# First attention of a four-part layer stack: the turned results, the state's chain and the turned states take other places in the step

## The reference

```
x: 16 batches of 256 tokens, 128 wide; 16 heads of 8
x = layernorm(x) * ln_w + ln_b
q, k, v = x @ Wq + bq, x @ Wk + bk, x @ Wv + bv      # per head
q, k = q / |q|, k / |k|
state = q
for _ in range(2):
    sim = einsum('bqhd,bkhd->bqhk', state, k)
    att = softmax(sim)
    state = einsum('bqhk,bkhd->bqhd', att, v)
return residual + state @ Wo + bo
```

## Time and profile before

| | |
|---|---|
| median of 3 runs | 1747.52 us (1744.76 to 1750.48) |
| profiled execution | 1759.47 us, span 1757.7 us |
| PE busy | 1489.7 us, 85% of the span |
| DVE busy | 1189.0 us, 68% |
| ACT busy | 1000.8 us, 57% |
| POOL busy | 785.2 us, 45% |
| first attention: first and last s0 or s1 | 59.2 to 559.7 us of the span |

### The profile page before, as it was taken

How to read it: one execution, slowest core, us unless ns; L and a number is a source line. 1 busy time by engine, 2 the same in 40 slices (tenths; PEclk the granted TensorE clock), 3 DMA queues, 4 the chain that set the end, 5 groups by cost and what they waited for, 6 DMA issues and landing times. The chain is left out here.

```text
span 1757.7 us, 37146 instructions
## 1 busy us (share of the span) xinstructions
PE 1489.7 (85%) x12057; PEld 1147.2 (65%) x12057; DVE 1189.0 (68%) x3253; ACT 1000.8 (57%) x1682; POOL 785.2 (45%) x1008
## 2 busy tenths in 40 slices
PE   2599999999999587999169998999899999689997
PEld 1467767767766466899046666666666666478886
DVE  2367777767766555999556777777777766556676
ACT  1377777777776254777126565665656666333332
POOL 8765464685662343998562334343333220100111
PEclk9899999999999788999569999999999999789999
DMA  5000000010010110222211111111111111000000
GB/s 192 21 20 19 16 19 17 25 32 19 25 35 19 33 58 12 73 68 64 77 42 35 35 35 40 31 35 33 33 33 33 31 30 30 1 1 7 12 12 18
DMA packets 75074, 60.29 MB, mean 34 GB/s; under 512 B 17088, under 2 KB 71104, under 8 KB 74560
## 3 DMA queue, kind: packets, MB, share of 16 engines
q1 hardware_dynamic: 70848, 50.21, 10.0%
q0 software_dynamic: 4096, 8.40, 1.7%
HBM read 20.01 MB, written 13.37 MB: 19 GB/s over the span
## 5 line engine op out<-in xcount | busy, mean ns | idle before, releaser
L1274 DVE TENSOR_REDUCE a_qt<-a_ps_d 128x2 fp32r<-128x512 f32 (+1 forms) x384 | 263.6, 689 | 140.8 <-PE a_ps_d L1059 96.3
L537 ACT ACTIVATE a_p<-a_ps_s 128x1024 f32<-128x1024 f32 x256 | 263.1, 1029 | 63.8 <-PE a_ps_s L395 59.4
L638 DVE TENSOR_REDUCE a_qt<-a_ps_d 128x2 fp32r<-128x512 f32 x256 | 171.6, 685 | 105.8 <-PE a_ps_d L406 105.5
L799 POOL TENSOR_TENSOR a_rn<-a_ss,a_half 128x16 f32<-128x16 f32 x64 | 185.9, 2913 | 1.4
L1186 ACT ACTIVATE a_pg<-a_ps_s 128x1024 f32<-128x1024 f32 x128 | 131.8, 1031 | 12.5 <-PE a_ps_s L1033 7.4
L1059 PE MATMUL a_ps_d<-a_kpad,a_qs 128*128 128x512 f32 x256 | 126.2, 493 | 13.6 <-DVE a_qt L1274 12.5
L406 PE MATMUL a_ps_d<-a_kpad,a_qs 128*128 128x512 f32 x256 | 119.7, 471 | 15.5 <-DVE a_qt L638 13.9
L413 PE MATMUL a_ps_o<-a_p,a_v 128*32 128x256 f32 x2048 | 125.3, 384 | 1.0 <-ACT a_p L537 1.0
L1024 PE MATMUL a_ps_a<-ident,a_qt 128*128 128x128 f32 x512 | 107.1, 291 | 10.8 <-ACT a_qsm L1180 8.0
L1505 POOL COPY a_v<-a_vt 128x64 f32<-128x64 f32 x64 | 15.4, 240 | 212.8 <-PE a_ps_o L1136 212.8
L1180 ACT CAST a_ks<-a_ps_a 128x256 fp32r<-128x256 f32 x128 | 47.6, 372 | 110.0 <-PE a_ps_a L1024 101.7
(11 more groups left out here) (359 smaller groups left out, 4280.1 us busy)
## 6 DMA issues: line engine op xcount, KB each, us to landing
a_kpad<-a_ks SPq DMA_DIRECT2D x512, 32.0 KB, 1.8
a_kpad<-a_kq SPq DMA_DIRECT2D x256, 32.0 KB, 1.9
f_xin<-xs SPq DMA_DIRECT2D x39, 128.0 KB, 2.1
ys<-f_yout SPq DMA_DIRECT2D x39, 128.0 KB, 2.1
w<-in_w SPq DMA_DIRECT2D x2, 2304.0 KB, 11.3
out_x<-X SPq DMA_DIRECT2D x8, 256.0 KB, 2.3
xs<-f_zero SPq DMA_DIRECT2D x15, 128.0 KB
wgu<-in_wgu SPq DMA_DIRECT2D x1, 1152.0 KB
```

The source lines that it names most:

```text
L537: nc.scalar.activation(probs[:, u % 2, 2 * c:2 * c + 2, :, :].rearrange("p a b c -> p (a b c)"), ps_s[:, n % 2, :], ACT.Exp).then_inc(exp_ ...
L638: nc.vector.tensor_reduce(qt2[:, k % 2, 2 * part:2 * part + 2, SHIFT], bank(k, f"m{part}")[:, :].rearrange("p (a b) -> p a b", b=S), AX.X, ...
L799: nc.gpsimd.tensor_tensor(rn[:, part * c:(part + 1) * c], ss[:, part * c:(part + 1) * c], half[:, 0:c], ALU.pow).then_inc(rn_ready, 1)
L1274: nc.vector.tensor_reduce(dst, src, AX.X, ALU.max, negate=True).then_inc(d_done, 1)
```

## The change

Three pieces of step k move; no instruction is added or removed.

- On TensorE T goes ahead of s1 (still behind s0 and qp).
- On TensorE O goes from behind m3 to behind KQ, ahead of vp and m2.
- On VectorE the chain of O goes from behind m3 to behind m1, ahead of vp, the two moments, m2 and m3. `D_ORDER` follows: O now takes its bank between m1 and vp (or m2).

```
--- before.py
+++ after.py
@@ -199,7 +199,7 @@
     FIRST, LAST = -3 * NG, UNITS + 3 * NG - 1
 
     A_ORDER = ("T", "KQ", "xT", "yT", "zT")
-    D_ORDER = ("qp", "m0", "lg", "place", "kp", "m1", "vp", "m2", "m3", "O", "op")
+    D_ORDER = ("qp", "m0", "lg", "place", "kp", "m1", "O", "vp", "m2", "m3", "op")
     KQ_RING = NG + 1
 
     def steps(eng):
@@ -444,8 +444,6 @@
                 if projects:
                     pe.wait_ge(a_done, a_count(k - 1, "xT"))
                     project(st, 0, "qp")
-                if unit(k):
-                    score_chunk(st, 1, kq[:, k % KQ_RING, 1, :])
                 if a_live(k, "T"):
                     pe.wait_ge(d_done, d_count(k - 1, "m3"))
                     wait_a(st, "T")
@@ -455,6 +453,8 @@
                     if unit(k - 3):
                         last = stack(lambda t: qt2[:, (k - 3) % 2, t * G:(t + 1) * G, :], 1)
                     last.then_inc(a_full, 1)
+                if unit(k):
+                    score_chunk(st, 1, kq[:, k % KQ_RING, 1, :])
                 if unit(k - 1) or unit(k - 4):
                     wait(pe, o_copied, attends(k - 1))
                     if unit(k - 4):
@@ -492,12 +492,6 @@
                     wait_a(st, "KQ")
                     stack(lambda t: kt[:, nb % 2, t * H + g * G:t * H + (g + 1) * G, :], 0)
                     stack(lambda t: qt[:, nb % 2, t * H + g * G:t * H + (g + 1) * G, :], 1).then_inc(a_full, 1)
-                if projects:
-                    project(st, 2, "vp")
-                maxima(st, 2)
-                if unit(k - 3):
-                    score_chunk(st, 3, qs2[:, S:2 * S])
-                maxima(st, 3)
                 if d_live(k, "O"):
                     wait_d(st, "O")
                     pe.wait_ge(o_copied, attends(k))
@@ -505,6 +499,12 @@
                     for n in range(live.start, live.stop, P):
                         last = nc.tensor.transpose(bank(k, "O")[:, n:n + P], ot[:, n:n + P], ident[:, :])
                     last.then_inc(d_full, 1)
+                if projects:
+                    project(st, 2, "vp")
+                maxima(st, 2)
+                if unit(k - 3):
+                    score_chunk(st, 3, qs2[:, S:2 * S])
+                maxima(st, 3)
                 if r == 2 and batch(b + 3):
                     pe.wait_ge(z1_ready, b + 4)
                     wait_a(st, "xT")
@@ -718,16 +718,6 @@
                     if not batch(b - 3):
                         last.then_inc(stats_b, 1)
                 maxima(1)
-                if r == 3 and batch(b + 3):
-
-                    wait(dve, v_ready, st.at(lambda k: NG * (k // NG + 2)))
-                    projected(st, 2, "vp", vt[:, (b + 3) % 2, :, :])
-                if r == 1 and batch(b - 3):
-                    moments(st, "new", 0, mv_b).then_inc(stats_b, 1)
-                if r == 0 and batch(b + 3):
-                    moments(st, "x", TPB, mv_a).then_inc(stats_a, 1)
-                maxima(2)
-                maxima(3)
                 if d_live(k, "O"):
 
                     dve.wait_ge(d_full, d_count(k, "O"))
@@ -758,6 +748,16 @@
                         dve.wait_ge(d_done, d_count(k, "O"))
                         nc.vector.tensor_tensor(new[:, :, 2 * HD:3 * HD], state[:, :, :],
                                                 new[:, :, 0:HD].bitcast(F32), ALU.subtract).then_inc(qt2_ready, 1)
+                if r == 3 and batch(b + 3):
+
+                    wait(dve, v_ready, st.at(lambda k: NG * (k // NG + 2)))
+                    projected(st, 2, "vp", vt[:, (b + 3) % 2, :, :])
+                if r == 1 and batch(b - 3):
+                    moments(st, "new", 0, mv_b).then_inc(stats_b, 1)
+                if r == 0 and batch(b + 3):
+                    moments(st, "x", TPB, mv_a).then_inc(stats_a, 1)
+                maxima(2)
+                maxima(3)
                 if r == 2 and batch(b - 2):
 
                     dve.wait_ge(d_full, d_count(k, "op"))
```

More of the change, by code:

```diff
@@ L494, in _ @@
                     stack(lambda t: qt[:, nb % 2, t * H + g * G:t * H + (g + 1) * G, :], 1).then_inc(a_full, 1)
[L495 to L500, removed]
                 if d_live(k, "O"):
@@ L720, in _ @@
                 maxima(1)
[L721 to L730, removed]
                 if d_live(k, "O"):
```

## The result

Before 1748.62 us (median of 4 runs, 1744.76 to 1750.48), after 1772.16 us (4 runs, 1771.08 to 1775.52): ratio 1.0141, 95% interval 1.0118 to 1.0164. The change makes the kernel 23.5 us slower; the prediction was 1769.0, 21.5 us slower, with a range of 1756 to 1781.

The account below looks back on a forecast made before the run. The prediction saw a loop of waits, with VectorE holding three T in four. 1.96 - 0.63 + 0.10 = 1.43 us per batch, times 15 batches, gave 21.5 us on a 1747.5 median: 1769.0 us, range 1756 to 1781.

Parts of the forecast that it names:

- s1 goes onto the loop: Between T and attend on TensorE: s1's four loads, hidden before, now cost 0.49 us per step, 1.96 per batch.
- m0 to T: Time from m0's start to T's in each step: 21.43 us per batch predicted, before 22.06.
- End 5.40, T 5.52: At r = 3: VectorE's reductions end 5.40 us after m0 and T starts at 5.52; before 5.79.
- T's copy comes no later with respect to T: ScalarE behind T: s1's chunk comes later, but T's copy was not to be delayed relative to T; no size given.
- the 0.63 us of gain: Between m0 and T: 0.63 us gained per batch from gaps in which VectorE waited.
- The moments on GpSimd: Moments behind O's chain reach GpSimd later; the scaling then delays r = 2's first reduction by 0.1 us per batch.
- few tenths: Three batches where scatters fill GpSimd: the later `stats_a` may add a few tenths of a us to each.
- The sum: Steps 4 to 63: 1.43 us more per batch, counted alike for 15 batches, 21.5 us.
- Faster: Rival: TensorE holds T in most steps, so T comes 0.49 us earlier per step; 1732 us, chance 0.07.
- Same: Rival: m0 to T shrinks by the price of s1, leaving time within 0.3%; 1750 us, chance 0.09.
- Much slower through GpSimd: Rival: late moments make the scaling delay r = 2's first reduction by 1 us or more; 1783 us, chance 0.08.
- a fall of the clock: Rival: longer TensorE idle time drops the clock to 1.2 GHz over the stage; about 1910 us, chance 0.01.

Follow-up runs that it names:

- e1: T alone moved ahead of s1 in the kernel before, O, its chain and `D_ORDER` unmoved: 1764.18 us, ratio 1.0098.
- e5: The changed kernel with the transposes zT right behind m0 and their copy ahead of the third exponential: 1770.49 us, ratio 1.0131.
- e6: The changed kernel with s3 ahead of m2: 1764.92 us, ratio 1.0101.
- e3: The changed kernel with VectorE's two moments ahead of O's chain again: 1767.03 us, ratio 1.0114.
- e4: The changed kernel with s1 ahead of T again and the moments ahead of O's chain: 1757.24 us, ratio 1.0057.
- e2: The changed kernel with s1 ahead of T again, so only O and its chain move: 1765.92 us, ratio 1.0108.
- e8: The kernel before with T cut in two, unit k-3's two transposes ahead of s1, the others behind: 1742.61 us, ratio 0.9972.
- e7: The changed kernel with moments ahead of O's chain, s3 ahead of m2, T cut in two around s1: 1747.37 us, ratio 0.9993.

## Why the prediction was right, point by point

*s1 goes onto the loop, 0.49 per step.* Right, and shown by e1: T to m0 grew from 2.45 to 2.92, at r = 3 to 0 from 2.50 to 2.98; 11.76 - 9.85 = 1.91 per batch for 1.96 predicted.

*m0 to T.* At r = 0 and 1 the walk along VectorE held: 5.26 and 5.29 predicted, 5.19 and 5.16 measured; T follows a reduction by 0.06 and not by 0.12, the lower of my two bounds. At r = 2 and 3 it failed: 5.36 and 5.52 predicted, 5.68 and 5.98 measured. The step of the prediction that failed at r = 3 is "End 5.40, T 5.52": I followed VectorE only and left out the other things for which T waits, the bank `ps_a`, and with it ScalarE's queue. "T's copy comes no later with respect to T" was beside the point; what stood ahead of T on ScalarE mattered (e5, e6). At r = 2 "op" was followed rightly: in the changed kernel it starts 453.75 - 449.43 = 4.32 after m0 instead of 4.00, 0.25 of it from the late first reduction. So the 0.63 us of gain came out as 0.05.

*The moments on GpSimd.* The mechanism was right, the size in ordinary batches 0.25 instead of 0.10. GpSimd itself kept to the forecast: `stats_b` comes 445.35 - 441.35 = 4.00 after its m0 and the scaling 4.26 behind it. What was off is the loop that hides it: r = 0 and r = 1 together took 16.20 us and not 16.43, so m0 of r = 2 was there sooner. The "few tenths" for the batches with scatters were 0.66 in steps 38 and 42 (first reduction 2.65 and 2.66 after m0, before 1.99 and 2.00), while in step 54 the wait shrank from 2.26 to 1.07. By e3 the moments' place is worth 4.7 us of the 23.5, with overlapping intervals, and by e4 against e2 8.7 where s1 doesn't lengthen the loop.

*The sum.* An ordinary batch costs 1.86 us more, not 1.43. That the total of 21.5 still came near 25.4 for the stage and 23.5 in the median is in part luck, two errors against each other: the first two batches cost 1.23 and 1.58, the last two 1.29 and 0.55, steps 52 to 55 nothing (-0.08), and I had counted all 15 alike; the two batches of steps 36 to 43 cost 2.29 and 3.61, the second with 1.3 of half clock.

*Rivals.* "Faster" needed m0 to T to shrink by 0.49 per step; it shrank by 0.01. "Same" falls with it. "Much slower through GpSimd" has the right mechanism at a quarter of its price. What I had not foreseen as a rival is that O's place costs in itself, 9.6 us in e4: 0.33 per batch at r = 2 through "op", which the prediction had seen but set against the 0.49 of s1, and 0.43 at r = 3 through m2's wait, s3 and the exponential, which it had not. The two halves don't add: 16.5 and 18.2 alone, 23.5 together. Per ordinary batch it is 1.40, 1.18 and 1.86. About a quarter of a microsecond of the difference lies at r = 2, where the scaling is less late in the longer loop (first reduction at 0.79 instead of 1.05); about 0.2 each lie at r = 1 and r = 3 and were not followed.

## What to carry to other kernels

A block that an engine does while it waits for another is free only in that place: before moving it behind the wait, ask whether the wait itself gets shorter by the block's length. When a step of a hand-ordered pipeline is moved, follow every semaphore of its new neighbours, also those of banks (m2 behind O's bank held s3, an exponential and a copy back), and the small signals that stand behind it for a third engine. Of a block that waits for two things, cut off the part that waits for the earlier one and do that first (e8), after a look at whose copy still holds its bank.

## What the runs showed of the hardware that was not expected

In the profiled execution of the changed kernel the clock fell once between step 4 and step 64. In step 42 (r = 2, with scatters) the weight loads stood still for 1.99 us ahead of O, and soon after TensorE was granted 1.2 GHz for a little over 3 us:

```profile
415.88 0.42 PEld L500 LDWEIGHTS a_ps_d<-ident,a_ot 128*128 128x128 f32 x4 [1.99 <-DVE a_qt L638]
```

```profile
378.00:382.00 4.00, 1.80 (x13) 1.28 (x12) 3.06 (x10) 1.36 (x2) 3.52 (x4) 1.00 0.18 44
414.00:418.00 4.00, 1.79 (x12) 1.39 (x11) 3.39 (x12) 0.99 (x3) 3.24 (x4) 1.00 0.16 41
418.20:421.40 3.20, 3.20 (x16) 2.83 (x15) 1.37 (x3) 2.92 (x5) 0.81 (x2) 0.50 0.06 17
```

The first row is step 38, which has the same wait of 1.99 us, the second is step 42. In both the matmul rows cover 1.8 of 4.00 us at full clock; only behind the second does the clock fall to 0.50 (third row). Step 42 took 11.85 us, step 38 10.51: 1.3 us. The kernel before has no such stretch in these steps. The prediction gave a fall of the clock 0.01 and priced it over the whole stage; it came in one place instead. Its "full level through the stage" holds from step 4 on; at the start of the stage, between 70 and 80 us, the kernel before had a clock of 0.50.

The Trainium skill, "TensorE: Matmul & The Clock Gate", Part 1, lets the clock follow how busy TensorE has lately been. The trace agrees in that the fall comes behind a long wait, but steps 38 and 42 waited alike and only one of them slowed down, so what tips it isn't shown here. Where such a fall comes differs between traces of nearly the same program: e2 and e5 have it in step 38 (in e5 11.86 us), e7 in steps 38 and 54, e8 in step 54, and e1, e3, e4 and e6 have none in steps 36 to 43. Each kernel has one trace, so whether the place is the kernel's or the execution's stays open.
